# A new order for the front of an attention and expert kernel: weights and tiles beside the router

## What is computed

```python
xn = layernorm(x)
q, k, v = xn @ Wq.T + bq, xn @ Wk.T + bk, xn @ Wv.T + bv
kv_sum = cumsum((elu(k) + 1) * v, axis=1)
s = ((elu(q) + 1) * kv_sum * SCALE) @ Wo.T + bo
top_p, top_i = top_k(softmax(xn @ router_w.T), 2)      # 256 places for each of 8 experts
g = silu(sum_k of top_p * (gelu(xn @ w1.T + b1) @ w2.T + b2))
out = x + s * g
```

## Time and profile before

| | |
|---|---|
| median of 3 runs | 1991.68 us (1990.5 to 1991.97) |
| the profiled execution | 1994.45 us, its span 1992.7 us |
| PE busy | 1950.5 us, 98% |
| DVE busy | 1377.3 us, 69% |
| ACT busy | 706.6 us, 35% |
| POOL busy | 512.7 us, 26% |
| mean granted clock of PE | 0.982 of 2.4 GHz |
| DMA | 416.27 MB, mean 209 GB/s |

### The profile page before, as it was taken

How to read it: one execution, slowest core, us unless ns; L and a number is a source line. 1 busy time by engine, 2 the same in 40 slices (tenths; PEclk the granted TensorE clock), 3 DMA queues, 4 the chain that set the end, 5 groups by cost and what they waited for, 6 DMA issues and landing times.

```text
span 1992.7 us, 27142 instructions
## 1 busy us (share of the span) xinstructions
PE 1950.5 (98%) x9374; PEld 900.7 (45%) x9374; DVE 1377.3 (69%) x2095; ACT 706.6 (35%) x1112; POOL 512.7 (26%) x643
## 2 busy tenths in 40 slices
PE   7999999999999999999999999999999999999996
PEld 2455555555444444444444444444444444444442
DVE  4887888888777776776777796564455465456656
ACT  2432222223644344335435442532212322322322
POOL 0058888888311321321310010210000000000002
PEclk6899999999999999999999999999999999999998
DMA  9547666667998988977776879673333233334535
GB/s 397 207 141 224 233 228 217 221 220 218 323 317 276 281 234 278 259 256 271 243 269 229 296 269 328 190 217 96 106 102 99 90 117 101 116 107 160 179 118 125
DMA packets 181308, 416.27 MB, mean 209 GB/s; under 512 B 17696, under 2 KB 70480, under 8 KB 178768
## 3 DMA queue, kind: packets, MB, share of 16 engines
q1 hardware_dynamic: 137696, 284.23, 43.0%
q0 software_dynamic: 34896, 121.71, 20.0%
q10 hardware_dynamic: 8608, 8.95, 1.4%
HBM read 268.51 MB, written 163.10 MB: 217 GB/s over the span
## 4 chain that ended last, share of the span: by engine, by line
PE 73%; POOL 12%; DMA 10%; issue 2%; DVE 2%; ACT 0%; SPq 0%; DVEq 0%; ACTq 0%; POOLq 0%
PE pair L2181 36%; PE pair L2152 35%; DMA arena<-w_down 3%; DMA arena<-w_up 3%; DMA arena<-x_t 2%; POOL arena L806 1%; POOL arena L817 1%; POOL arena L810 1%; POOL arena L811 1%; POOL arena L808 1%; POOL arena L794 1%; POOL arena L821 1%; POOL arena L822 1%; POOL arena L819 1%; POOL up_sums L800 1%
## 5 line engine op out<-in xcount | busy, mean ns | idle before, releaser
L2181 PE MATMUL pair<-arena 128*128 128x512 f16 x3360 | 730.1, 379 | 1.1 <-DVE arena L1728 0.5
L2152 PE MATMUL pair<-xnT,arena 128*128 128x512 f16 x2400 | 525.2, 379 | 3.3 <-ACT xnT L1068 2.0
L2181 PEld LDWEIGHTS pair<-arena 128*128 128x128 f16 x3360 | 327.8, 98 | 400.1 <-issue 7.0
L1720 DVE SCALAR_TENSOR_TENSOR arena<-pair,arena 128x1024 f32<-128x1024 f32 x234 | 285.9, 1222 | 151.0 <-PE pair L2181 150.1
L1987 PE MATMUL pair<-arena 128*128 128x512 f16 x1728 | 382.9, 379 | 0.9 <-DVE arena L1351 0.7
L1143 ACT ACTIVATE arena<-arena 128x512 f16<-128x512 f32 x280 | 171.4, 626 | 555.3 <-PE pair L2181 500.6
L2152 PEld LDWEIGHTS pair<-xnT,arena 128*128 128x128 f16 x2400 | 234.3, 98 | 287.9 <-ACT xnT L1068 3.5
L1987 PEld LDWEIGHTS pair<-arena 128*128 128x128 f16 x1728 | 168.6, 98 | 194.5 <-ACT arena L927 1.6
L2152 PE MATMUL pair<-xnT 128*128 128x512 f16 x960 | 213.7, 379 | 0.0
L1695 DVE SCALAR_TENSOR_TENSOR arena<-arena 128x512 f16<-128x512 f32 x280 | 189.1, 688 | 16.4 <-ACT arena L1143 15.7
L849 POOL DMA_DIRECT2D s_dram<-arena x8 | 6.2, 776 | 596.4 <-DVE arena L1720 596.4
(11 more groups left out here) (217 smaller groups left out, 1803.1 us busy)
## 6 DMA issues: line engine op xcount, KB each, us to landing
down_dram<-arena SPq DMA_DIRECT2D x70, 512.0 KB, 7.0
arena<-down_dram SPq DMA_DIRECT2D x70, 512.0 KB, 3.3
up_dram<-arena SPq DMA_DIRECT2D x90, 256.0 KB, 5.8
arena<-up_dram SPq DMA_DIRECT2D x90, 256.0 KB, 2.6
arena<-down_sums SPq DMA_DIRECT2D x40, 512.0 KB, 6.2
arena<-w_up POOLq DMA_DIRECT2D x36, 512.0 KB, 5.3
up_sums<-arena POOLq DMA_DIRECT2D x36, 512.0 KB, 3.7
arena<-up_sums SPq DMA_DIRECT2D x67, 256.0 KB, 4.9
```

Source lines behind the costliest of these rows:

```text
L1720: ins = nc.vector.scalar_tensor_tensor(to, src, scale, to, ALU.mult, ALU.add)
L2152: ins = mm(out_to, w[:, a, c * P:(c + 1) * P], x_in_op[:, b, c, :], start=(first and i == 0), stop=(i == 11), skip_group_check=True)
L2181: ins = mm(down_banks(j, t // 2)[:, (t % 2) * BLOCK:(t % 2 + 1) * BLOCK], g_ops[:, A_NAMES.index(DOWN_A[j]), c, a, t * P:(t + 1) * P], dow ...
```

## The change

The change rewrites the front on all five queues. x of tile 0 is loaded first, then x_t in halves with the chunks of w_kv between them, seven stages for chunks in place of nine; all chunks are asked for before block 4 of x_t. Tiles 0, 1 and 2 are turned by products with ident, and their kept columns selected by separate products later (`keep_x`); before, this was so for tile 0 alone, and `select_x` did both at once for the others. Tile 0 is projected chunk by chunk as the low parts of weights arrive (`arriving`), tile 1 between the halves of blocks 4 to 7, tile 2 after the router. The biases of k and v are loaded as one row each and spread over the partitions by four fp32 products and two copies of ACT; before, two DMAs did this. Tiles 2 and 3 stand outside the loop, which starts at pair 2. POOL's sums start behind keep_x(2). Tile 0 has a buffer of its own for phi(k) * v (`kv_first`), tile 2 one for its split x (`x_hl_third`). The core of the diff, without the bodies that only became functions; between `scores_by_token(4)` and the block 7 lines PE's list goes on in the same pattern, two chunks of tile 1 and then a half or the products by token:

```diff
-WL = 9
+WL = 7
...
-xt_in = [part(2 + 4 * u, 4).rearrange("p (c t) -> p c t", c=CH) for u in range(2)]
-EARLY, SOON = TOKEN_BLOCKS - 2, TOKEN_BLOCKS + 1
-kv_stage = ([xnT_f[:, 1024 * c:1024 * (c + 1)] for c in range(EARLY)]
-            + [xnT_f[:, 13824 + 1024 * c:13824 + 1024 * (c + 1)] for c in range(SOON - EARLY)]
-            + [part(n, 1) for n in (12, 13, 10, 11, 14, 15, 16)])
+xt_in = [xnT_f[:, 4 * 1024 * u:4 * 1024 * (u + 1)].rearrange("p (c t) -> p c t", c=CH) for u in range(2)]
+kv_stage = [xnT_f[:, 13824 + 1024 * c:13824 + 1024 * (c + 1)] for c in range(3)] + [part(n, 1) for n in (10, 11, 14, 15)]
+kv_first = part(16, 1).bitcast(F16).rearrange("p (h e) -> p h e", h=2)
+x_hl_third = part(14, 1).bitcast(F16).rearrange("p (h d) -> p h d", h=2)
...
-    return bank[0][:, u * BLOCK:u * BLOCK + n].rearrange("p (t e) -> p t e", e=EXPERTS + 1)
-TRANSPOSED, KEPT = (bank[1], bank[3]), (bank[2], bank[3])
+    return bank[3][:, u * BLOCK:u * BLOCK + n].rearrange("p (t e) -> p t e", e=EXPERTS + 1)
+TRANSPOSED, KEPT = ((bank[0], bank[1]), (bank[0], bank[0]), (bank[0], bank[0])), (bank[2], bank[3])
...
-    def load_wkv(q):
-        if q >= WL:
-            sp.wait_ge(wkv_ready, q - WL + 1)
-        sp.dma_start(kv_stage[q], w_kv[q]).then_inc(wkv_loaded[q % WL], 16)
-    sp.dma_start(xt_in[0][:, 0:2, :], x_t[0][:, 0:2, :]).then_inc(xt_first, 16)
-    sp.dma_start(xt_in[0][:, 2:4, :], x_t[0][:, 2:4, :]).then_inc(xt_loaded[0], 16)
+    def load_wkv(*qs):
+        for q in qs:
+            if q >= WL:
+                split_ready(sp, q - WL)
+            sp.dma_start(kv_stage[q % WL], w_kv[q]).then_inc(wkv_loaded[q % WL], 16)
+    def load_x(t):
+        if t >= 2:
+            sp.wait_ge(kxlo_ready, t - 1)
+        sp.dma_start(x_in[t % 2], x_tiles[t]).then_inc(kx_loaded[t % 2], 16)
+    load_x(0)
+    load_xt(0, 0)
     load_xt(0, 1)
+    load_wkv(0, 1, 2)
     load_xt(1, 0)
+    load_wkv(3, 4, 5)
     load_xt(1, 1)
-    for u in range(2):
-        sp.dma_start(x_in[u], x_tiles[u]).then_inc(kx_loaded[u], 16)
-    load_wkv(0)
-    for b, weights in ((2, (1, 2)), (3, (3, 4)), (4, (5, 6)), (5, (7, 8)), (6, (9,)), (7, (10, 11, 12, 13, 14, 15))):
+    load_wkv(6, 7)
+    load_x(1)
+    load_wkv(8, 9)
+    load_xt(2, 0)
+    load_wkv(10)
+    load_xt(2, 1)
+    load_wkv(11, 12)
+    load_xt(3, 0)
+    load_wkv(13)
+    load_xt(3, 1)
+    load_wkv(14, 15)
+    load_x(2)
+    for b in range(4, TOKEN_BLOCKS):
         for half in range(2):
             load_xt(b, half)
-            for q in weights[half::2] if b < TOKEN_BLOCKS - 1 else weights * half:
-                load_wkv(q)
-    sp.wait_ge(wkv_ready, SOON + 1)
-    sp.dma_start(bk_row, b_k.to_broadcast((P, D))).then_inc(rows_loaded, 16)
-    sp.wait_ge(wkv_ready, SOON + 2)
-    sp.dma_start(bv_row, b_v.to_broadcast((P, D))).then_inc(v_row_loaded, 16)
+    load_x(3)
...
-    def tile(t, u):
-        sp.wait_ge(kxlo_ready, t + 1)
-        apart(sp)
-        sp.dma_start(x_in[u], x_tiles[(t + 2) % TILES]).then_inc(kx_loaded[u], 16)
+    def tile(t, u, loads=True):
+        if loads:
+            sp.wait_ge(kxlo_ready, t + 1)
+            apart(sp)
+            sp.dma_start(x_in[u], x_tiles[(t + 2) % TILES]).then_inc(kx_loaded[u], 16)
...
-        tile(t, t)
-    with sp.Fori(1, pairs) as g:
+        tile(t, t, loads=False)
+    for t in range(2, 4):
+        tile(t, t % 2)
...
-    pool.wait_ge(scores_done, TOKEN_BLOCKS)
-    nc.gpsimd.memset(kv_hl[:, :, :], 0.0).then_inc(kvlo_ready, 2)
-    pool.wait_ge(wkv_ready, 12)
+    pool.wait_ge(wkv_ready, 11)
...
-    pool.wait_ge(wkv_ready, 2 * CH)
-    pool.wait_ge(tables_ready, 2)
...
+    pool.wait_ge(front_done, kept_in(2, LO))
...
-    pool.wait_ge(kvlo_ready, 6)
...
-            if u >= 1:
+            if u == 0:
+                pool.wait_ge(stage_done, 10)
...
+    act.dma_start(bk_row[0:1, :], b_k).then_inc(rows_loaded, 16)
+    act.dma_start(bv_row[0:1, :], b_v).then_inc(rows_loaded, 16)
...
+    act.wait_ge(rows_spread, 1)
+    for row, pair in ((bk_row, bank[1]), (bv_row, bank[0])):
...
+    ins.then_inc(rows_ready, 1)
+    high_x(0, 1, x_hl[0])
+    copy_scores(0)
+    copy_turned(0, HI)
+    copy_turned(0, LO)
+    high_wkv(0, 1, 2, 3, 4, 5)
+    copy_scores(1)
+    high_wkv(6, 7, 8, 9)
+    exp_k(0, 0)
+    exp_k(0, 1)
+    high_wkv(10)
+    high_x(1, 2, x_hl[1])
+    copy_scores(2)
+    high_wkv(11)
+    copy_turned(1, HI)
+    high_wkv(12)
+    copy_turned(1, LO)
+    high_wkv(13)
+    copy_scores(3)
+    high_wkv(14, 15)
+    high_kv(0, kv_first)
+    copy_scores(4)
+    copy_scores(5)
+    split_ready(act, 12)
+    high_x(0, 3, x_hl_third)
+    copy_scores(6)
+    exp_k(1, 0)
+    exp_k(1, 1)
+    copy_scores(7)
+    copy_turned(2, HI)
+    copy_turned(2, LO)
...
+    copy_kept(0, slice(0, P))
...
+    copy_kept(1, ds(at, P))
+    high_kv(1, kv_hl)
...
+        act.dma_start(win_dram[:, :, ds(at_n, P)], window[0]).then_inc(tail_stored, 16)
+    at = act.value_load(start_i[0:1, 3:4], min_val=0, max_val=SLOTS)
+    copy_kept(2, ds(at, P))
...
+    high_x(1, 4, x_hl[1])
...
+    for t in range(2, 4):
+        tile(t, t % 2)
...
+    def choose(b):
...
+    stats_x(0, 1, 16)
+    norm_x(0, 0, 1)
+    dve.wait_ge(sums_w_done, 1)
+    own.link(nc.vector.tensor_scalar(rw_sum[:, :], out_bank(7)[:, 0:EXPERTS], -1.0 / D, None, ALU.mult))
+    low_x(0, 1, x_hl[0])
+    choose(0)
+    low_wkv(*range(CH))
+    choose(1)
+    dve.wait_ge(rows_ready, 1)
+    read_k(0, 0)
+    read_k(0, 1)
+    low_wkv(8, 9)
+    phi_k(0)
+    stats_x(1, 2, 16)
+    norm_x(1, 1, 2)
+    choose(2)
+    low_wkv(10, 11)
+    low_x(1, 2, x_hl[1])
+    low_wkv(12, 13)
+    choose(3)
+    low_wkv(14, 15)
+    times_v(0)
+    choose(4)
+    low_kv(0, kv_first)
+    stats_x(0, 3, 32)
+    norm_x(0, 2, 3)
+    choose(5)
+    low_x(0, 3, x_hl_third)
+    choose(6)
+    read_k(1, 0)
+    read_k(1, 1)
+    choose(7)
+    phi_k(1)
...
+    def tile(t, u, g, third=False):
...
+    for t in range(2):
+        ins = places(t, t)
+    ins.then_inc(tables_ready, 1)
+    dve.wait_ge(front_done, kept_in(0, LO))
+    kept_columns(0, 2).then_inc(select_ready, 1)
+    times_v(1)
+    low_kv(1, kv_hl)
+    stats_x(1, 4, 32)
+    norm_x(1, 3, 4)
+    dve.wait_ge(front_done, kept_in(1, LO))
+    kept_columns(1, 3)
+    sums(1, 1, 9, steps=3)
+    low_x(1, 4, x_hl[1])
+    tile(2, 0, 1, third=True)
+    tile(3, 1, 1)
...
+    def arriving(v, *chunks, first=0):
+        for c in chunks:
+            split_ready(pe, CH * v + c)
+            for n in (2 * v, 2 * v + 1):
+                project_chunks(0, n, (c,), first=first)
+    pe.wait_ge(zeros_ready, 1)
...
+    pe.wait_ge(pool_consts, 2)
+    pe.wait_ge(rows_loaded, 32)
+    for row, pair in ((bk_row, bank[1]), (bv_row, bank[0])):
+        for half in range(2):
+            e = slice(half * BLOCK, (half + 1) * BLOCK)
+            ins = mm(pair[:, e], ones_f[0:1, :], row[0:1, e], start=True, stop=True)
+    ins.then_inc(rows_spread, 1)
+    pe.wait_ge(zeros_ready, 2)
+    half_scores(0, 0)
+    pe.wait_ge(zeros_ready, 3)
+    mm(out_bank(7)[:, 0:EXPERTS], ones_f, rw_chunks[:, :, 0], start=True, stop=True).then_inc(sums_w_done, 1)
+    half_scores(0, 1)
+    pe.wait_ge(const_ready, 1)
+    pe.wait_ge(rows_ready, 1)
+    pe.wait_ge(kxhi_ready, 1)
+    turn(0, HI, x_hl[0])
+    pe.wait_ge(zeros_ready, 4)
+    scores_by_token(0)
+    pe.wait_ge(kxlo_ready, 1)
+    turn(0, LO, x_hl[0])
+    pe.wait_ge(front_read, turned(0, LO))
+    arriving(0, 0)
+    half_scores(1, 0)
+    arriving(0, 1, 2, 3, 4)
+    half_scores(1, 1)
+    arriving(0, 5)
+    scores_by_token(1)
+    arriving(0, 6, 7)
+    half_scores(2, 0)
+    arriving(1, 0, 1)
+    half_scores(2, 1)
+    scores_by_token(2)
+    arriving(1, 2, 3)
+    pe.wait_ge(proj_read, 4 + 2)
+    pe.wait_ge(kxhi_ready, 2)
+    turn(1, HI, x_hl[1])
+    half_scores(3, 0)
+    pe.wait_ge(front_read, turned(1, HI))
+    pe.wait_ge(kxlo_ready, 2)
+    turn(1, LO, x_hl[1])
+    arriving(1, 4)
+    half_scores(3, 1)
+    arriving(1, 5)
+    scores_by_token(3)
+    pe.wait_ge(front_read, turned(1, LO))
+    project_chunks(1, 0, range(0, 4))
+    half_scores(4, 0)
+    project_chunks(1, 0, range(4, 7))
+    arriving(1, 6, 7)
+    half_scores(4, 1)
+    project_chunks(1, 0, range(7, CH))
+    scores_by_token(4)
...
+    project_chunks(1, 2, range(4, 6))
+    half_scores(7, 0)
+    project_chunks(1, 2, range(6, CH))
+    half_scores(7, 1)
+    project_chunks(1, 3, range(0, 1))
+    scores_by_token(7)
+    pe.wait_ge(proj_read, 4 + 6)
+    pe.wait_ge(kxlo_ready, 3)
+    turn(2, HI, x_hl_third)
+    project_chunks(1, 3, range(1, 4))
     pe.wait_ge(chosen_ready, TOKEN_BLOCKS)
     picks = chosen[:, :, :, :].rearrange("p k e t -> p (k e t)")
...
     mm(out_bank(4), before[:, :], picks, start=True, stop=True)
     mm(out_bank(5), ones[:, :], picks, start=True, stop=True).then_inc(places_ready, 1)
+    pe.wait_ge(front_read, turned(2, HI))
+    turn(2, LO, x_hl_third)
+    project_chunks(1, 3, range(4, CH))
```

(42 more changed lines are left out.)

437 lines of the change are left out of this document (160 added, 277 removed).

## The result

The changed kernel is slower: 2014.99 us median against 1991.83 us of the kernel before on the same chip. Its single executions in all runs but the odd one lie between 2008.3 and 2018.1 us, those of the kernel before between 1990.5 and 1996.8. I forecast 2002.7, so the direction was right and the size was half: +11 us against +21 (by the ratio) to +24.

What follows compares the result with a forecast made beforehand. Time was taken as the front up to 66 us plus TensorE's own work. Work and queue waits put tile 3 at 150.2 us against 139.2, +11.0 us, so 2002.7 us median; range 1989 to 2014.

Steps and rivals of the forecast that it cites:

- The mark: PE's first product of tile 3: at 139.2 us before the change, forecast at 150.2 us after it.
- M: PE's first product of tile 3's second output, a point read after measuring: 145.72 us before, 165.57 us after.
- Step a: From the start to PE's first weight chunk, forecast at 20.9 us.
- Step b: From the first weight chunk to chunk 2 of W_v at 52.3 us; VectorE becomes the chain, PE waits 12.5 us.
- Step c: From chunk 2 of W_v to the counts of kept rows at 110.5 us; PE the bound, 50.9 us work, waits 5.3.
- Step d: From the counts to tile 3 at 150.2 us; VectorE the chain, PE waiting some 14 us for its reads.
- 2.3 if the clock never falls a second time: Before tile 3: its start at 151.5 us would come 2.3 us earlier without a second clock fall; 150.2 was taken.
- Nothing behind gives it back: After tile 3's start: the +11.0 us lost in the front was to reach the end whole.
- (4): Rival: clock stays low in the front until 66 us, tile 3 at 158 to 162, time 2011 to 2015; chance 0.12.
- (1): Rival: faster, as waits before tile 3 overlap; over 0.2% only with waits under 20 us, 1985 with half; chance 0.12.
- (2): Rival: no change; clock stays at 2.4 GHz and tile 4's x lands in time; 1991 to 1995 us; chance 0.14.
- signs of being wrong: Tile 3 before 135 us, PE idle under 20; or granted clock 0.5 past 60; or new PE waits behind 160.

Runs made afterwards that it cites:

- e4: The changed kernel with VectorE's own reads of tile 2 moved ahead of the statistics and norm of tile 4's x: 2007.05 us, ratio 1.0072.
- e5: The changed kernel with VectorE's statistics and norm of tile 1 put between low parts 5 and 6: 2007.10 us, ratio 1.0079.
- e8: The changed kernel with the zero tail's store moved ahead of tile 1's kept-column copies and high parts of kv on ScalarE's queue: 2008.46 us, ratio 1.0067.
- e1: The changed kernel profiled again without any edit: 2010.27 us, one execution.
- e11: The changed kernel without any edit, timed a second time on another chip: 2016.24 us, ratio 1.0110 to the kernel before.
- e12: On top of e9, norms of tiles 2, 3 and 4 moved into VectorE's gaps, tile 3's x loaded behind block 4 of x_t: 1995.92 us, ratio 1.0011.
- e9: The changed kernel with bias rows by DMA, tile 1's norm early, tail store early, tile 4's x ahead and tile 2's reads first: 1996.09 us, ratio 1.0016.

## Why the prediction was right in direction and half in size

The mark came 6.1 us later than forecast, 0.4 + 1.3 + 1.5 + 3.0 by steps a to d (windows above), M 8.8 us later. The term that was mis-sized is PE's work at the lower clock level: 9 us more between the first chunk and M, 2.7 in step b, 3.3 in c, 0.3 in d and 2.7 in tile 3.

- **Where PE goes idle: right.** The wait for block 2's scores behind the norm in ScalarE's queue (forecast near 42 us, seen at 48.90, 4.95 us), low part 10 behind it, the statistics of tile 4 waiting for DMA (forecast 7 us, 5.6 seen), PE's waits for the odd copies (forecast 14 us, 13.7 seen), and none on x_t behind the first chunk. e4, e5 and e8 each took away or shortened one of these and got the time.
- **Step a, 20.9 us: the spread was undersized.** I priced it at 3.5 us, four products of 0.9 at the upper level, and let the clock fall near 11.6. It takes 5.31 us in e1, 7.06 in e11, and PE waits 1.6 to 2.8 us for the rows ahead of it: the clock falls in or before it, at another moment in each execution. That the first chunk still came only 0.4 us late in e1 is luck: PE's transposes of tile 0 began 2.7 us later than in my working (15.55 against 12.8) but took 2.3 us with the products by token between them, where I had 5.0, as they ran at the upper level; in e11 the chunk was 2.9 us late. This may be one reason why the times of the change spread over 10 us; no run shows it.
- **Step b, 52.3 us: waits 12.5, seen 11.1; the work had no clock in it.** I priced 18.9 us of work, it took 21.6. The clock is at 0.50 in 22 to 24 us, so the first six products take 2.11 us and the half of scores behind them 1.94 instead of 1.47 and 1.07, and again from 50 us on.
- **Step c, 110.5: waits 5.3, seen 3.5; work 52.9, seen 56.2.** The 2 us that I gave the clock went into the 12 products at 53.98 alone, which take 5.30 us instead of 2.76. A further fall, at 80 us behind a wait of 1.59, had no price: six products take 2.72 us there.
- **Step d, 150.2: VectorE's chain, not PE's clock, made it late.** Tile 4's x landed 28.3 us behind the counts, as forecast (28.4). The chain from there took 14.3 us where I had 12.6 (last section), and 1.3 us more are my own: I took 150.2, between 151.5 and 149.2, for the chance that the clock would not fall a second time. It fell, and so the discount was wrong. The two make the 3.0 us. PE's slow products before 156.33 lie inside the time in which it would have waited for VectorE, and cost nothing.
- **Tile 3: my "2.3 if the clock never falls a second time" stopped at the second fall.** The wait of 10.45 us brought one more, which was not priced:

```profile
140.00:150.00 10.00, 0.48 (x3) 0.36 (x4) 7.09 (x17) 1.70 (x4) 8.13 (x13) 0.57 1.00 377
150.00:160.00 10.00, 6.79 (x18) 2.33 (x17) 9.93 (x13) 2.34 (x4) 9.08 (x11) 0.50 0.56 184
```

  It reaches 2.7 us into tile 3, past my mark. In e12, where no wait over 1.4 us is left from 74 to 140 us, the clock is 1.00 from 80 on and the 24 take 5.34.
- **What ties the work to the waits.** From first chunk to M the same products are busy 113.0 us in e11, 108.1 in e4, 107.1 in e9, 106.4 in e12: removing 16.6 us of idle time (32.6 to 16.1) took 6.6 us of work along. That is a comparison of kernels that differ in other ways too; the one direct trial, the products in the wait, gained nothing, so this share of the cause is argued and not shown. The Trainium skill (TensorE: Matmul & The Clock Gate, HAM oscillation) says that waits for data between bursts of products let the clock fall again each time. With that rule the trace of e1 agrees in part: the clock is at 0.50 behind the waits of 3.41, 4.95 and 10.45 us, and also behind those of 1.59 and 2.34, but stays at 1.00 behind those of 0.73 and 1.89 between 34 and 43 us. My text used the rule for the second fall only.
- **"Nothing behind gives it back": wrong, by 4 us.** The kernel before had waits between 514 and 568 us that a later TensorE does not meet. The error is of the other sign and hid part of the first.
- **Rivals.** (4), clock low until 66, named the size (2011 to 2015) but not the mechanism: the clock is at 1.00 in 30 to 45 us. (1) needed waits of under 20 us; e12 has 16.1 and its front is faster than before, so its condition was right and not met by the change. (2) is refuted by the clock and by VectorE's wait of 5.63 us for x of tile 4. One of my own signs of being wrong came: a granted clock of 0.50 past 60 us, in 80 to 82, 128 to 130 and 142 to 156. The other two did not: PE was idle for 31 us, and behind 165 no new wait above 0.3 us came.

## What to carry to other kernels

Price a wait of the array twice: its length, and the products behind it at half speed; here 6.6 us of busy time went with 16.6 us of waits. The second price counts only where PE itself sets the pace: where it waits for another engine next, as in step d, slow products fill the wait. When a reordering loses, look in each queue for a ready instruction behind one that waits for another engine or a load (a norm ahead of copies, a store behind them, reads behind statistics): four such moves, and the bias rows by DMA, brought 20 us back with the new structure kept. Try such moves together before adding up their gains: one by one they came to 35. Look also at what is issued just ahead of a store on which a chain hangs: behind two loads of POOL it took 7.6 us to land, ahead of them 3.3. And before gaining time in a front, find the next floor (here POOL's sums and waits at 510 to 570 us), since it decides what arrives.

## What was not expected

- **One execution at a sixth of the speed.** The profile taken with the result shows every product of 512 columns 1.32 us from the next (4448.3 us / 3360) instead of 0.22, all through, with the recorded clock at 1.000, while VectorE's instructions keep their length (L1763 1225 ns against 1223). It was the only one of its kind:

```profile
L2283 PE MATMUL pair<-arena 128*128 128x512 f16 x3360 | 4448.3, 1706 | 0.0
```

  The Trainium skill (TensorE: Matmul & The Clock Gate, Part 1) warns that the clock's records are at times not to be trusted; a record of full speed beside products of six times the length agrees with that. The cause stays open.
- **The record can say 1.00 while the array runs at half.** In e4 the clock is recorded as 1.00 from 0 to 20 us, and the spread takes 7.16 us and a half of the scores 1.94, the length it has at the lower level. Durations are the safer witness.
- **Small VectorE instructions stretch when POOL adds.** In e1 the root's steps of one column take 0.55 to 0.70 us from 144.8 on, while POOL adds, 0.16 to 0.22 otherwise, some 1.8 us in the chain of tile 4. I had 12.6 us for that chain and it took 14.3 (141.94 to 156.24), so this term was slightly low.
